# Token numbers carried in the sorted rows: tile results scattered to token order instead of stored and gathered

## The reference

```python
scores = jnp.einsum('btd,ed->bte', x, Wg)
topk_s, topk_i = jax.lax.top_k(scores, TOP_K)          # TOP_K = 2
probs = jax.nn.softmax(topk_s, axis=-1)
...
for e in range(E):                                      # E = 8
    h = jax.nn.silu(jnp.einsum('btd,hd->bth', x, W1[e])) * jnp.einsum('btd,hd->bth', x, W2[e])
    y = y + w[..., e:e + 1] * jnp.einsum('bth,dh->btd', h, W3[e])
```

## Time and profile before

| | us |
|---|---|
| median of 3 runs (lowest, highest) | 1227.72 (1225.61, 1229.09) |
| time of the profiled execution | 1230.84 |
| its span | 1229.1 |
| last tile result written by ACT | 1188.97 from the start of the span |

### The profile page before, as it was taken

One profiled execution on the slowest core, in us unless ns is written; L12 is line 12 of the kernel. 1 busy time (PEld: TensorE's weight loads), 2 busy tenths in 40 slices (PEclk: granted clock), 3 DMA queues, 4 the chain that ended last, 5 costly groups with the idle time before them and its releaser, 6 DMA issues.

```text
span 1229.1 us, 27499 instructions
## 1 busy us (share of the span) xinstructions
PE 1083.4 (88%) x8482; PEld 890.7 (72%) x8482; DVE 730.3 (59%) x1989; ACT 576.2 (47%) x1254; POOL 441.5 (36%) x602
## 2 busy tenths in 40 slices
PE   3799999999998889999999999999888898999960
PEld 3566676676675678888888888888876777777740
DVE  3557767767665165556666666666764556756733
ACT  2145555455454334455544544455563445545530
POOL 4234344344342112122333333333652112315615
PEclk8669999999998789999999999999995999999985
DMA  7434444444442074001111111112142222435644
GB/s 231 123 112 133 117 125 133 115 123 136 118 120 88 2 244 133 23 23 31 41 42 42 42 42 42 42 42 64 66 138 82 74 78 94 130 122 172 199 142 149
DMA packets 98292, 122.17 MB, mean 99 GB/s; under 512 B 16022, under 2 KB 85852, under 8 KB 98204
## 3 DMA queue, kind: packets, MB, share of 16 engines
q1 hardware_dynamic: 91292, 102.17, 27.7%
q0 software_dynamic: 6912, 18.88, 4.7%
HBM read 64.37 MB, written 56.10 MB: 98 GB/s over the span
## 4 chain that ended last, share of the span: by engine, by line
PE 62%; DVE 15%; ACT 9%; issue 7%; POOL 3%; DMA 2%; SPq 1%; DVEq 1%; ACTq 0%; POOLq 0%
PE bank L947 5%; PE bank L1617 4%; PE bank L853 3%; PE bank L1619 3%; PE bank L1618 3%; DVE a_negm L1302 3%; PE bank L855 2%; PE bank L854 2%; PE bank L607 2%; PE bank L979 2%; PE bank L624 2%; PE bank L636 2%; PE bank L626 2%; PE bank L625 2%; PE bank L1630 2%
## 5 line engine op out<-in xcount | busy, mean ns | idle before, releaser
L1178 ACT ACTIVATE a_prob<-bank 128x512 f32<-128x512 f32 x192 | 114.2, 598 | 141.7 <-PE bank L947 141.3
L1617 PE MATMUL bank<-b_xF_hi,wff_hi 128*128 128x256 f32 x512 | 153.9, 301 | 2.2 <-DVE b_xF_lo L1993 1.4
L1302 DVE TENSOR_REDUCE a_negm<-bank 128x2 f32<-128x512 f32 (+1 forms) x192 | 129.5, 684 | 39.9 <-PE bank L914 39.9
L1619 PE MATMUL bank<-b_xF_hi,wff_lo 128*128 128x256 f32 x512 | 145.6, 284 | 0.0
L1618 PE MATMUL bank<-b_xF_lo,wff_hi 128*128 128x256 f32 x512 | 145.6, 284 | 0.0
L1426 POOL TENSOR_SCALAR_AFFINE_SELECT a_prob<-a_prob 128x1024 f32<-128x1024 f32 x64 | 70.0, 1094 | 176.9 <-ACT a_prob L1178 176.9
L947 PE MATMUL bank<-a_Q,a_K 50*128 50x256 f32 (+1 forms) x512 | 111.5, 322 | 1.9 <-DMA a_Q<-bias_rows 1.5
L914 PE MATMUL bank<-a_K,a_Q 48*128 48x128 f32 (+1 forms) x512 | 108.0, 320 | 0.0
L947 PEld LDWEIGHTS bank<-a_Q,a_K 50*128 50x128 f32 x512 | 76.1, 199 | 40.4 <-issue 28.8
L1617 PEld LDWEIGHTS bank<-b_xF_hi,wff_hi 128*128 128x128 f32 x512 | 98.1, 192 | 7.5 <-DVE b_xF_lo L1993 1.8
L2001 DVE TENSOR_TENSOR b_hf<-bank,b_sg 128x256 f32<-128x256 f32 x128 | 54.0, 422 | 80.2 <-ACT b_sg L1845 77.6
(11 more groups left out here) (270 smaller groups left out, 3160.7 us busy)
## 6 DMA issues: line engine op xcount, KB each, us to landing
scr<-a_split SPq DMA_DIRECT2D x64, 256.0 KB, 2.4
a_Q<-scr SPq DMA_DIRECT2D x192, 64.0 KB, 2.2
a_K<-scr SPq DMA_DIRECT2D x192, 64.0 KB, 2.3
m_xs<-x_sorted SPq DMA_DIRECT2D x78, 128.0 KB, 2.1
y_sorted<-m_y SPq DMA_DIRECT2D x78, 128.0 KB
x_sorted<-b_r_zeros SPq DMA_DIRECT2D x1, 6016.0 KB, 20.0
parts<-b_split SPq DMA_DIRECT2D x16, 256.0 KB, 2.1
out<-x_res SPq DMA_DIRECT2D x16, 256.0 KB, 2.8
```

Source lines behind the costliest of these rows:

```text
L1178: nc.scalar.activation(o, src, ACT.Exp, scale=float(HD) ** -0.5).then_inc(S.exps, 1)
L1302: nc.vector.tensor_reduce(R.negm[:, p, j, c0:c0 + n], ps[bank][:, :].rearrange("p (h k) -> p h k", h=n), axis=AX.X, op=ALU.max, negate=Tru ...
L1617: pe.matmul(o, wh, xh, start=(c == 0), stop=False)
L1619: mm = pe.matmul(o, wl, xh, start=False, stop=(c == NC - 1))
```

## The change

Every row of `x_sorted` becomes one float wider (`ROW` = 257) and carries the token's number, which is the row that its result gets in a new tensor `y_token`. GpSimd writes the number behind the normed row, for choice 0 and then, when that is out, for choice 1, so `p_scatter` is in two halves. A tile is loaded with its numbers (now seven buffers `m_xs`), and its result goes by an indirect DMA of POOL straight to token order. The sums load `y_token` with plain DMAs issued by SP, 256 rows each. Fills and spare rows come from a constant `c_pad`, whose numbers point behind the real rows; SP issues them. Part 2 of the table, the copy of the row numbers, and all gathers are gone. The adds of group 0 begin at step 54 instead of 53.

```diff
-        self.rows = NEXP * self.cap + self.tiles * P
+        self.rows = NEXP * (self.cap + P)
...
-                nc.vector.tensor_copy(R.rows[:, cols(s * 4, 4)].rearrange("p (c j) -> p c j", c=2), rows)\
-                    .then_inc(S.chain, 1)
...
+            def p_scatter(pool, s, p, c):
+                if c == 0:
+                    pool.wait_ge(S.chain, s * LINKS + LINKS - 1)
+                else:
+                    pool.wait_ge(S.scattered[p], (s - p) * 32 + 32)
                 plain(pool)
+                nc.gpsimd.tensor_copy(R.xn[p][:, :, E].bitcast(I32), R.ids[:, cols(s * 4 + 2 * c, NT)]).then_inc(S.named, 1)
+                pool.wait_ge(S.named, s * 2 + c + 1)
+                plain(pool)
+                for j in range(NT):
+                    n = NT * c + j
+                    nc.gpsimd.indirect_dma_start(
+                        out=x_sorted, out_offset=bass.IndirectOffsetOnAxis(ap=R.row[p][:, n:n + 1].bitcast(U32), axis=0),
+                        in_=R.xn[p][:, j, :], in_offset=None).then_inc(S.scattered[p], 16)
+
+            def sp_fill(sp, g):
+                sp.wait_ge(S.ends, g + 1)
                 for e in range(NEXP):
+                    first = sp.value_load(R.fill[0:1, g, e:e + 1], min_val=0, max_val=SORTED - P)
+                    sp.dma_start(x_sorted[bass.ds(first, P), :], c_pad[(2 * NEXP * g + e) * P:(2 * NEXP * g + e + 1) * P, :]).then_inc(S.filled, 16)
...
+            XS = 7
+            FIRST_SUM = TOKENS[1].tile + 7
+
+            def sum_load(eng, s, c):
+                n = 2 * s + c
+                if n >= 4:
+                    eng.wait_ge(S.added, 2 * (n - 3))
+                rows = y_token[(c * NSEQ + s) * T:(c * NSEQ + s + 1) * T, :].rearrange("(j p) e -> p j e", p=P)
+                eng.dma_start(R.ring[:, 2 * (n % 4):2 * (n % 4) + 2, :], rows).then_inc(S.gathered[s % 2], 16)
...
             def sp(eng):
...
+                for i in range(NTILES):
...
+                    if i == 41:
+                        route.sp_fill(eng, 1)
...
                     row = eng.value_load(R.table[0:1, 2, i:i + 1], min_val=0, max_val=SORTED - P)
                     if i >= 4:
                         eng.wait_ge(S.xT_ps, i - 3)
+                    if i >= XS:
+                        k = i - XS
+                        eng.wait_ge(S.stored[k % 3], 16 * (uses(k, k % 3, 3) + 1))
+                    eng.dma_start(R.xs[:, i % XS, 0:ROW], x_sorted[bass.ds(row, P), :]).then_inc(S.loaded[i % 4], 16)
+                    n = i - FIRST_SUM - 3
+                    if 0 <= n < 2 * split:
+                        if n == 0:
+                            all_scattered(eng, TOKENS[1].tile)
+                        s, c = divmod(n, 2)
+                        if c and s >= 3:
+                            out_store(eng, s - 3)
+                        sum_load(eng, s, c)
+                for s in range(split - 3, split):
+                    out_store(eng, s)
+                all_scattered(eng, NTILES)
+                for s in range(split, NSEQ):
+                    for c in range(2):
+                        sum_load(eng, s, c)
+                    if s > split:
+                        out_store(eng, s - 1)
+                out_store(eng, NSEQ - 1)
...
-                eng.wait_ge(S.gathered[s % 2], 64 * (s // 2 + 1))
+                eng.wait_ge(S.gathered[s % 2], 32 * (s // 2 + 1))
...
+            def pool(eng, k):
+                if 0 <= k < NTILES:
+                    eng.wait_ge(S.y, k + 1)
+                    nc.gpsimd.indirect_dma_start(
+                        out=y_token, in_=R.y[:, k % 3, :], in_offset=None,
+                        out_offset=bass.IndirectOffsetOnAxis(ap=R.xs[:, k % XS, E:E + 1].bitcast(U32), axis=0))\
+                        .then_inc(S.stored[k % 3], 16)
...
+            def p_tile_step(pool, t, p):
+                for m in range(NM):
+                    X1["pool"](pool, tile_of(t, m) - 3)
...
+                    if m == 3 and live(t - 4):
+                        route.p_ln(pool, t - 4)
+                    if m == 4:
+                        if live(t - 3):
+                            p_causal(pool, t - 3)
+                        if live(t - 5):
+                            route.p_scatter(pool, t - 5, 1 - p, 0)
+                    if m == 6 and live(t - 1):
+                        p_rope(pool, t - 1)
+                    if m == 7 and live(t - 5):
+                        route.p_scatter(pool, t - 5, 1 - p, 1)
```

More of the change, by code:

```diff
@@ L478, in uses @@
                 return len(range(k, n, depth))
-            LINKED = (7, 12, 7)
-            CLEARED = sum(LINKED[:2]) + 2
-            COUNT = {(g, part): g * sum(LINKED) + sum(LINKED[:part]) + 2 * ((g, part) >= (0, 2)) for g in range(2) for part in range(3)}
+            LINKED = (7, 12)
+            CLEARED = sum(LINKED) + 2
+            COUNT = {(g, part): g * sum(LINKED) + sum(LINKED[:part]) + 2 * g for g in range(2) for part in range(2)}
             NARROW = 18
@@ L555, in sp, with out_store, all_scattered @@
+            def out_store(eng, s):
+                eng.wait_ge(S.added, 4 * s + 4)
+                dst = out.rearrange("b (j p) e -> p (b j) e", p=P)
+                eng.dma_start(dst[:, 2 * s:2 * s + 2, :], x[:, 2 * s:2 * s + 2, :]).then_inc(S.out, 16)
+            def all_scattered(eng, tiles):
+                for k in range(3):
+                    eng.wait_ge(S.stored[k], 16 * uses(tiles, k, 3))
             def sp(eng):
-                for i in range(NTILES + 8):
+                split = GROUPS[0][1]
+                for i in range(NTILES):
@@ L561, in sp @@
                         layer["sp_step"](eng, NSEQ + 1, 1)
-                    if i < NTILES:
-                        for g, grp in enumerate(TOKENS):
-                            if i == grp.tile:
-                                eng.wait_ge(S.table, g + 1)
-                                for p in range(2):
-                                    eng.wait_ge(route.S.scattered[p], 64 * ((grp.seqs[1] + 1 - p) // 2))
-                                eng.wait_ge(route.S.filled, NEXP * 16 * (g + 1))
-                        if i == 0:
-                            eng.wait_ge(layer["S"].up, NSEQ * INTER0 // P)
-                        row = eng.value_load(R.table[0:1, 2, i:i + 1], min_val=0, max_val=SORTED - P)
-                        if i >= 4:
-                            eng.wait_ge(S.xT_ps, i - 3)
-                        eng.dma_start(R.xs[:, i % 4, :], x_sorted[bass.ds(row, P), :]).then_inc(S.loaded[i % 4], 16)
@@ L575, in sp @@
-                    n = i - 8
-                    if n >= 0:
-                        eng.wait_ge(S.y, n + 1)
-                        g = sum(n >= grp.tile for grp in TOKENS[1:])
-                        first = (n - TOKENS[g].tile) * P
-                        eng.dma_start(y_sorted[g][first:first + P, :], R.y[:, n % 3, :]).then_inc(S.stored[n % 3], 16)
-                dst = out.rearrange("b (j p) e -> p (b j) e", p=P)
-                for s in range(NSEQ):
-                    eng.wait_ge(S.added, 4 * s + 4)
-                    eng.dma_start(dst[:, 2 * s:2 * s + 2, :], x[:, 2 * s:2 * s + 2, :]).then_inc(S.out, 16)
+                    if i == 41:
+                        route.sp_fill(eng, 1)
@@ new lines, in sp @@
+                    for g, grp in enumerate(TOKENS):
+                        if i == grp.tile:
+                            eng.wait_ge(S.table, g + 1)
+                            for p in range(2):
+                                eng.wait_ge(route.S.scattered[p], 64 * ((grp.seqs[1] + 1 - p) // 2))
+                            eng.wait_ge(route.S.filled, NEXP * 16 * (g + 1))
+                    if i == 0:
+                        eng.wait_ge(layer["S"].up, NSEQ * INTER0 // P)
+                    row = eng.value_load(R.table[0:1, 2, i:i + 1], min_val=0, max_val=SORTED - P)
@@ L773, in dve @@
                     eng.wait_ge(route.S.weights, NSEQ)
-                if i >= TOKENS[1].tile + 6:
+                if i >= FIRST_SUM:
                     for _ in range(2):
@@ L2303, in run @@
                         return
-                    step(eng, t, t % 2)
-                if engine != "pool":
-                    for i in range(tile_of(last, NM - 1) + 1, NTILES + 2):
-                        X1[engine](eng, i)
+                    if engine == "pool" and t >= NSEQ:
+                        p_tile_step(eng, t, t % 2)
+                    else:
+                        step(eng, t, t % 2)
+                behind = tile_of(last, NM - 1) + 1
+                for i in range(behind, NTILES + (3 if engine == "pool" else 2)):
+                    X1[engine](eng, i - 3 if engine == "pool" else i)
             return dict(S=S, run=run, v_f_ln=v_f_ln, p_f_ln=p_f_ln, sp_step=sp_step)
```

111 lines of the change are left out of this document (33 added, 78 removed).

## The result

The changed kernel takes 1243.16 us, the median of four runs (1240.54 to 1247.26), against 1228.40 for the kernel before (1225.61 to 1233.40): 1.0134 of its time, 95% interval 1.0101 to 1.0167. It was forecast at 1223.5, faster by 4.2; it is slower by 14.8 us. In a later group of runs the pair took 1243.33 (1238.55 to 1248.79) and 1227.87: ratio 1.0140, interval 1.0074 to 1.0205.

A forecast was written before the change was run, and what follows sets the result against it. TensorE was taken as 62% of the chain of waits, the sums bounding the tail; −17.5 + 7 + 2.4 + 3.2 + 1.7 (clock) − 1.0 = −4.2 took the median 1227.72 to 1223.5 us, range 1212 to 1234.

The forecast's parts named there:

- The sums of group 0: Steps 54 to 73: ring loads behind result landings make VectorE wait, TensorE loses 1.4 per pair of sequences; cost 7 us.
- I take 2.6 since the DMA share stays as it was: Sums' path: scatter and 256 KB load each land in 2.6 us, with DMA share staying at 0.53.
- the prediction's own rule: Sums of group 0: each us of path beyond the assumed 6.0 costs 5 us more.
- the 1.0 us waits of the sums should not: Sums of group 0: TensorE's 1.0 us waits should not bring the low clock, unlike two new waits over 2 us.
- Rival C: Sums' path longer, landings 3.5 each: stage costs 9 more, low clock once per pair 4.3; total +9, 1237; chance 0.16.
- Tile 31: Step 19 beside the attention: POOL's list delays result 24's scatter, so tile 31 loads late; cost 2.4 us (0 to 5).
- Elsewhere in these steps the same count leaves the loads 1 us or more: Tile steps beside the attention: apart from tile 31, loads keep a margin of 1 us or more.
- The fills: Eight fills of group 1 on SP, 1.1 us each, ahead of tile 41's load; cost 3.2 us (0 to 8).
- The tail: Behind the last tile result: plain loads replace 24 gathers, sequence 15's adds begin at +18.1 instead of +35.6; gain 17.5 us.
- D: Rival: tail loads behind stores land in 4 us or more, two sequences take 7; gain 12, time 1229; chance 0.08.
- E: Rival: wide rows move in uneven pieces, each landing 1 to 2 us later; +4, time 1228; chance 0.07.
- Small edits: Dropped part 2 of the table and 16 dropped VectorE copies, in the attention steps: gain 1.0 us (0 to 3).

The follow-up runs named there:

- the kernel with late stores: Changed kernel with sums' loads two tiles earlier, fills issued singly, POOL's norm and first sorted pair later, ten output stores behind the last tile load: 1216.76 us.
- the one with the deep ring: Against the kernel with late stores: seven ring loads in flight in the tail instead of four, stores three sequences behind their loads; 1212.37 us.

## Why the prediction was wrong, step by step

**The sums of group 0: forecast 7, measured 24.6.** This is the step that failed. The path from a result to the add was put at 6.0; in the changed kernel it is 7.9 in the mean of the ten sequences: 0.28 until POOL starts, 3.48 from there to the tile's load, 0.78 to the ring's load, 3.32 to its landing. Two terms are off. "I take 2.6 since the DMA share stays as it was": it did stay, 0.54, and the landings were 3.2 to 3.3 all the same, since a mean share doesn't say how close the transfers stand together; tile load, store and ring load are issued within 1.5 us of a landing. The row that was nearest is that of the stores in a row, 2.8 to 5.5. And the output store that SP issues between the tile's load and the ring's, from sequence 3 on, was counted in the tail but left out here. By the prediction's own rule, 5 us for each us of path, 7.9 gives 7 + 9.5 = 16.5, and TensorE's idle time did grow by 16.7. The rest is the low clock, 6.9, which "the 1.0 us waits of the sums should not" bring: VectorE's waits of every second sequence came to 4.1 to 5.2 us, TensorE's to 3.0 to 4.2, and its clock fell in every round. The 2 us that the prediction names for POOL's scatters beside a busy VectorE didn't come: they took 958 to 961 ns each.

**Rival C was right** in its size here, 7 + 9 + 4.3 = 20.3, in the long landings and in the clock that falls once per pair, and had a chance of 0.16. Why the landings were long, whether the transfers queue on one another as C says, no run separates. What spoke against it, the share of 0.53 and the medians of landings of lone transfers, didn't bear on it. The Trainium skill (HBM Reference, section "Latency") gives 2 us for an access under high load; the ring's landings were 0.7 us longer in the mean than the forecast's 2.6, and no run here shows what part of a landing the access is. The stage needs no such load to lose 20 us.

**Tile 31: forecast 2.4 and up to 0.85 for the clock, measured 6.3.** Result 24's scatter started when it was forecast (the changed kernel is 9.6 us ahead there: 1042.0 + 9.6 = 1051.6, forecast 1051.3). It landed after 4.45 us, not 2.5; it was issued right behind two sorted scatters that themselves took 3.0 and 3.7. The maximum of the earlier trace rows, 4.0, was the nearer row. SP then took 0.5 us to issue the load, not 0.1. The copy of the numbers with its waits took 1.03 us (1038.47 to 1039.50), not 0.6. "Elsewhere in these steps the same count leaves the loads 1 us or more" was wrong for tile 30 by the prediction's own numbers: result 23 goes at 1047.1, lands at 1049.6, and tile 30's rows are there at 1051.8, while TensorE wanted them at 1050.89 in the kernel before. It waited for them in both profiles, 1.3 and 3.7 us.

**The fills: forecast 3.2, measured 6.6 with the clock.** A fill takes 1.31 us of SP (1073.30 to 1082.47, seven intervals), not 1.1: its issue takes 0.53 where a tile's load takes 0.34. The wait was 5.8 us and brought the low clock, as forecast for a wait of over 2 us.

**The tail: forecast 17.5, measured 14.9,** within its bounds of 14 to 19. From result 77 at 1215.61 to the first add are 6.4 us (forecast 5.8), from sequence 10 to 12 to 14 5.7 and 5.8 (forecast 5.3). D and E fell; from 1040 to 1100 us the wide rows land like the narrow ones, in 2.1 us in the median.

**Small edits: forecast 1.0 of gain, measured 2.6** in the attention steps alone. Results 0 to 26 look like another 3.4 us of gain in the table. The profiles don't settle it: seven of kernels with the change need 103.4 to 108.0 us there, mean 105.5, against 107.4 before, but the four on the chip where the kernel before was slow need 110.4 to 113.8.

Put together: 24.6 + 6.3 + 6.6 - 14.9 - 2.6 - 0.2 behind the last add = +19.8 for the pieces that repeat; the medians say 14.8 and 15.5, the second group's interval 9 to 25. Some 5 us of gain are thus unexplained, of which results 0 to 26 may be 2. By the same pieces the kernel with late stores comes to -11.5 and measures -11.1, the one with the deep ring to -16.7 and -15.5. The range 1212 to 1234 failed for one reason above all: the sums' path and tile 31's were priced by landings near the medians of lone transfers, the fills by the issue of a tile's load, and all three erred the same way. That the tail stayed in its bounds didn't help: its gain was 2.6 smaller as well.

## What to carry to other kernels

Where a load is released by the landing of a result that its own consumer holds up, price the loop, not the wait: path plus the time back to the next result, against the steps that it has to fit in. Take the landings for such a path from rows of transfers issued in a row, not from a median over lone ones, and don't infer them from the mean DMA share. A wait on one semaphore for two loads asks for the later one at the date of the earlier; a semaphore each, or an issue one or two steps ahead, won back 17 to 20 of the 24.6 us here without moving a byte less.

## What was not expected of the hardware

TensorE's register loads from a table in SBUF took up to 0.7 us where the DMA share was 0.71 (loads two tiles earlier), and 0.30 to 0.39 at a share of 0.65 with the output stores gone. SP's were long in the first of these kernels too, 485 ns in the mean, and 340 without the stores, against 270 before the change. What this costs in time is open, as said above.

After waits of 1.8 and 1.2 us TensorE's clock stayed at 1.2 GHz for 31 us (from 49.5 us on), of which TensorE worked 29.5, in one execution; after 1.7 and 1.0 us it came back after 3.4 us in another of the same program (0.56 and 0.86 mean granted clock over the same 35 us). The runs of one kernel differ by 3 to 15 us; how much of that is the clock wasn't measured.

On one chip the kernel before took 1255.86 us instead of some 1228, and the edited versions run beside it did not show such a difference in their pieces, except that results 0 to 26 took 110 to 114 us there and 103 to 108 elsewhere. The cause wasn't found.
